# Normalising the attention probabilities of both layers on GpSimd, with a second product by a power of two

## What is computed

```python
q_hk = (hidden_q @ Wq.T).reshape(b, s, H, K)
q_big = jnp.einsum('bshk,hkq->bshq', q_hk, w_kc_q)   # layer 0 also turns q_big by its position
q_r = jnp.einsum('bshq,hqr->bhsr', q_big, W_qr)
k_r = jnp.einsum('bld,hdr->bhlr', kv_rope, W_kr)
scores = jnp.einsum('bhsr,bhlr->bhsl', q_r, k_r)
attn = jax.nn.softmax(scores, axis=-1)
ctx_c = jnp.einsum('bhsl,bld->bhsd', attn, kv_rope)
ctx_lat = jnp.einsum('bhsd,hkd->bshk', ctx_c, w_kc_kv)
out = ctx_lat.reshape(b, s, H * K) @ Wo.T
```

## Time and profile before

| | us |
|---|---|
| median of three runs | 1126.4 |
| lowest and highest | 1124.43, 1128.03 |
| the profiled execution | 1128.36 |
| its span on the core | 1126.6 |

### The profile page before, as it was taken

The page is one execution under the profiler, slowest core; times in us unless marked ns, Lnnn a source line. Parts: engine busy times, 40 slices in busy tenths (PEclk is TensorE's granted clock), DMA queues, the critical chain, the costliest instruction groups (busy, mean ns, idle before and its releaser), DMA issues. The chain is left out here.

```text
span 1126.6 us, 19728 instructions
## 1 busy us (share of the span) xinstructions
PE 989.5 (88%) x6194; PEld 577.9 (51%) x6202; DVE 745.8 (66%) x1315; ACT 542.8 (48%) x1224; POOL 525.5 (47%) x518
## 2 busy tenths in 40 slices
PE   0679999999999998899567569999999988998998
PEld 0335555555555555444233245776777764444543
DVE  3768777777877776396688527888888884323112
ACT  1355656565665656100467316677767673105400
POOL 2968999899899989100233203333333331110000
PEclk9999999999999999999879769999999999999999
DMA  7112121303212110350300002121221003204000
GB/s 218 56 43 66 44 72 36 98 19 98 64 43 65 42 28 21 140 190 35 112 10 19 29 9 71 62 65 65 65 65 59 6 1 140 75 1 159 0 29 37
DMA packets 24191, 69.23 MB, mean 61 GB/s; under 512 B 3162, under 2 KB 5338, under 8 KB 21719
## 3 DMA queue, kind: packets, MB, share of 16 engines
q1 hardware_dynamic: 18656, 58.01, 15.4%
q10 hardware_dynamic: 5492, 10.67, 3.5%
HBM read 64.99 MB, written 3.67 MB: 61 GB/s over the span
## 5 line engine op out<-in xcount | busy, mean ns | idle before, releaser
L819 ACT ACTIVATE scratch<-ps,mxn 112x375 f32<-112x375 f32 x256 | 144.2, 571 | 61.5 <-DVE mxn L940 61.5
L1086 POOL TENSOR_SCALAR scratch<-scratch,rinv 112x375 f32<-112x375 f32 x128 | 164.3, 1293 | 17.0 <-DVE rinv L945 16.7
L1203 PE MATMUL ps<-arena 128*128 128x512 f16 x672 | 147.8, 382 | 2.3 <-PEq L600 2.3
L1075 POOL CAST scratch<-scratch 128x375 f16<-128x375 f32 x128 | 67.1, 524 | 174.3 <-ACT scratch L846 174.3
L940 DVE TENSOR_REDUCE mxn<-ps 112x2 f32<-112x750 f32 x128 | 119.2, 931 | 17.8 <-PE ps L633 17.4
L684 PE MATMUL ps<-xnT,scratch 128*128 128x448 f16 x576 | 124.0, 362 | 3.8 <-DVE scratch L1023 2.4
L671 PE MATMUL ps<-scratch,kvn_hi 125*128 125x224 f16 x768 | 119.9, 260 | 6.8 <-DVE scratch L994 4.7
L656 PEld LDWEIGHTS ps<-ident,scratch 112*125 112x125 f32 x768 | 99.9, 188 | 46.1 <-issue 34.8
L1078 POOL TENSOR_TENSOR scratch<-scratch 128x375 f16<-128x375 f32 x128 | 115.3, 901 | 10.6
L656 PE MATMUL ps<-ident,scratch 112*125 112x112 f32 x768 | 106.7, 275 | 13.7 <-DVE scratch L1014 9.2
L1068 POOL TENSOR_TENSOR scratch<-scratch 128x896 f32<-128x896 f32 x64 | 104.4, 1633 | 27.2 <-DVE scratch L972 26.3
(11 more groups left out here) (138 smaller groups left out, 1538.0 us busy)
## 6 DMA issues: line engine op xcount, KB each, us to landing
scratch<-in_wq SPq DMA_DIRECT2D x16, 512.0 KB, 5.3
scratch<-in_wo SPq DMA_DIRECT2D x16, 512.0 KB, 3.6
wabs<-in_w ACTq DMA_DIRECT2D x32, 256.0 KB, 3.0
scratch<-in_w SPq DMA_DIRECT2D x8, 1024.0 KB, 4.9
scratch<-in_W SPq DMA_DIRECT2D x8, 1024.0 KB, 6.2
scratch<-in_kcq SPq DMA_DIRECT2D x8, 512.0 KB, 5.4
scratch<-in_qr SPq DMA_DIRECT2D x32, 128.0 KB, 3.6
scratch<-in_kcq SPq DMA_DIRECT2D x8, 384.0 KB, 3.3
```

Of the source, the lines that this page charges most:

```text
L819: last = nc.scalar.activation(prob[0:S, s % 2, hh, :], scores_ps[0:S, hh, 0:L], ACT.Exp, bias=mxn[0:S, s % 2, hh:hh + 1], accum_out=rsum[0 ...
L1086: last = nc.gpsimd.tensor_scalar(prob[0:S, s % 2, hh, :], prob[0:S, s % 2, hh, :], rinv[0:S, s % 2, hh:hh + 1], None, ALU.mult)
L1203: last = nc.tensor.matmul(ps[:, b, :], a[:, h, ds(t * P, P)], c[:, h, :], start=(h == 0 and i == 0), stop=(h == H - 1 and i == 2))
```

## The change

In layer 1 NORM leaves VectorE and goes to GpSimd, ahead of K in its list, so that GpSimd normalises in both layers. In both layers GpSimd's instruction now makes two products in one pass, by the reciprocal and by 2^14. The factor 2^14 is taken out of the two instructions behind the transposes: ScalarE's copy has no scale any more, and VectorE's low half becomes a plain difference of two operands.

```diff
 GPSIMD (layer 1)
-    [("K", 2)], [("K", 3)], [("K", 4)], [("K", 5)],
...
+    [NORM, ("K", 2)], [NORM, ("K", 3)], [NORM, ("K", 4)], [NORM, ("K", 5)],
...
 turned_out (ScalarE)
                             probT_hi[0:LP, s % 2, :].rearrange("p (c n) -> p c n", c=LC),
-                            turn_ps[0:LP, :, 0:2 * S], ACT.Copy,
-                            scale=P_SCALE).then_inc(turn_high, 1)
+                            turn_ps[0:LP, :, 0:2 * S], ACT.Copy).then_inc(turn_high, 1)
 reciprocals (VectorE)
-                        if layer == 0:
-                            return
-                        dve.wait_ge(recip_done, nth(p, B, s))
-                        for hh in range(2):
-                            last = nc.vector.tensor_scalar(
-                                prob[0:S, s % 2, hh, :], prob[0:S, s % 2, hh, :],
-                                rinv[0:S, s % 2, hh:hh + 1], None, ALU.mult)
-                        last.then_inc(prob_done, 1)
 turned_low (VectorE)
-                        nc.vector.scalar_tensor_tensor(
+                        nc.vector.tensor_tensor(
                             probT_lo[0:LP, s % 2, :].rearrange("p (c n) -> p c n", c=LC),
-                            turn_ps[0:LP, :, 0:2 * S], P_SCALE,
+                            turn_ps[0:LP, :, 0:2 * S],
                             probT_hi[0:LP, s % 2, :].rearrange("p (c n) -> p c n", c=LC),
-                            ALU.mult, ALU.subtract).then_inc(turn_out, 1)
+                            ALU.subtract).then_inc(turn_out, 1)
 normalise (GpSimd)
                             last = nc.gpsimd.tensor_scalar(
                                 prob[0:S, s % 2, hh, :], prob[0:S, s % 2, hh, :],
-                                rinv[0:S, s % 2, hh:hh + 1], None, ALU.mult)
+                                rinv[0:S, s % 2, hh:hh + 1], P_SCALE, ALU.mult, ALU.mult)
```

More of the change, by code:

```diff
@@ L138 @@
 ], [
-    [("K", 2)], [("K", 3)], [("K", 4)], [("K", 5)],
-    [("K", 6)], [("K", 7)], [("K", 0)], [("K", 1)],
+    [NORM, ("K", 2)], [NORM, ("K", 3)], [NORM, ("K", 4)], [NORM, ("K", 5)],
+    [NORM, ("K", 6)], [NORM, ("K", 7)], [NORM, ("K", 0)], [NORM, ("K", 1)],
 ])
```

## The result

The changed kernel takes 1123.87 us in the median of 14 executions (1120.14 to 1126.12) where the kernel before takes 1126.62 (14 executions, 1124.43 to 1131.51): a ratio of 0.9963, with 95% between 0.9953 and 0.9974. The ratio makes it some 4.2 us; the two medians by themselves are 2.8 us apart. Measured a second time, unaltered, it gave 0.997 (0.9957 to 0.9983; experiment 7). The forecast was 9.9 us. The time lies inside the range, but less than half of the forecast gain is there.

A forecast was written before the change was run, and what follows sets the result against it. TensorE sets the pace, with GpSimd close behind in layer 0 and VectorE in layer 1. Terms 2.1 + 6.0 + 1.0 + 0.8 = 9.9 us took the median from 1126.4 to 1116.5; range 1112 to 1127.

The forecast's parts named there:

- The instruction: GpSimd's NORM instruction with two products, 375 elements: 0.52 us, between 0.36 and 0.89, where one product takes 1.29.
- Rivals 1 and 2: GpSimd's two-product instruction keeps its price: 1126 us, chance 0.13; or pays for each product: about 1340, with milder forms 0.10.
- rival 1: GpSimd's instruction keeps its price; layer 1's last slots take 3.86 us, last transposes 0.8 later; 1126 us, chance 0.13.
- Layer 0, middle pairs: Six middle pairs of layer 0: TensorE does not wait for NORM, so a quicker GpSimd changes nothing, 0 us.
- Layer 0, the end: Last pair of layer 0: slots shrink from 3.86 to 3.35 us and last transposes start 0.8 earlier, 2.1 us gained.
- Layer 1: Layer 1 without NORM on VectorE: 6.0 us from the pairs, 1.0 at the start, 0.8 in the last pair.
- The pair: Each pair of layer 1 shortens by 0.91 us through three slots, for 7 pairs, some weaker: 6.0 us.
- slot 6: Layer 1, where Q's halves stand behind NORM on VectorE: TensorE starts S earlier, 0.33 us back a pair.
- W's slot: Layer 1, three VectorE products between NORM and the low half: 0.28 us back a pair.
- the slot with U: Layer 1, slot behind slot 6: VectorE would start U's low half 0.25 us earlier, 0.30 back a pair.
- The other two edits: Factor removed from VectorE's difference out of PSUM and scale from ScalarE's copy, both layers: 0 us.
- own range: Whole kernel: 1112.5 to 1121 us, allowing a third of layer 1's gain lost or another 3 us of hidden stalls.

The follow-up runs named there:

- experiment 7: The whole change measured a second time, unaltered, against the kernel before: 1124.37 us against 1127.33, ratio 0.997.
- experiment 3: NORM on GpSimd in both layers with one product, factor 2^14 kept behind the transposes, against the kernel before: 1130.73 us, ratio 1.0027.
- experiment 4: Two kernels without the model, copying the input and running GpSimd's forms alone and beside VectorE's split: one product of 375 columns 1.22 us, two products 0.59.
- experiments 1 and 2: The change in layer 0 alone: 1127.18 us, ratio 1.0004; the change in layer 1 alone: 1122.41 us, ratio 0.996; both against the kernel before.
- 5 for the path: VectorE's second weight split moved behind the maxima in the changed kernel: 1113.24 us; moved ahead of U instead: 1114.0; behind the maxima in the kernel before: 1120.2.

## Why the prediction was wrong, point by point

**The instruction** was forecast at 0.52 us, between 0.36 and 0.89; it takes 0.59 undisturbed, 0.62 in the mean. The reading that the two-operation form is the cheap one held, for two products too. Rivals 1 and 2 fell with it, and experiment 3 shows that rival 1 had the slots at the end of layer 1 right (3.86 us), but not what is lost behind them (2.6 us until the projection starts, where it had 0.8). By the rule of the Trainium skill, "GPSIMD Engine Reference", section "Elementwise — side-by-side cycle accounting", one and two operations cost the same; experiment 4 has 1.22 against 0.59 us, which contradicts it.

**Layer 0, middle pairs: the failed step.** The prediction says "In the middle pairs TensorE waits for VectorE and ScalarE there and not for NORM, so I count 0 (the cover is TensorE's own work, 97%)". The first half was true and should have been the alarm. TensorE waited for VectorE once in each pair, so whatever makes VectorE later there costs the path at once. The step asked only whether a quicker GpSimd gives something back, and took no change to be the worst case. But it moves every GpSimd instruction behind NORM earlier, onto another instruction of VectorE. The cost is 0.37 us in six pairs and 0.15 in the first, 2.4 us in all (experiments 1 and 2 for where it comes from, 4 for the mechanism, 5 for the path). A middle pair that grows was in none of the rivals.

**Layer 0, the end** was forecast at 2.1 us and gave 2.2: the last slots went to 3.35, 3.36 and 3.35 us (1.34) and the last transposes came 0.84 earlier. No scores wait for GpSimd any more, as said.

**Layer 1.** 7.8 us were forecast, 6.5 came. The start gave 1.04 for 1.0, the end 0.76 for 0.8. The pair gave 0.69 of 0.91: slot 6 gave 0.35 for 0.33, W's slot 0.31 for 0.28, and the slot with U 0.04 for 0.30. This last term was mis-sized. It took VectorE to start U as soon as ScalarE is through. ScalarE (858) and VectorE (980), first in the loop, then in the pair that is written out:

```profile
771.83 0.62 ACT L858 ACTIVATE arena<-ps 128x512 f32 x1
```

```profile
772.71 0.69 DVE L980 SCALAR_TENSOR_TENSOR arena<-ps,arena 128x512 f32 x1 [0.92 <-ACT arena L858]
```

```profile
708.24 0.61 ACT L858 ACTIVATE arena<-ps 128x512 f16<-128x512 f32 x1
```

```profile
708.89 0.69 DVE L980 SCALAR_TENSOR_TENSOR arena<-ps,arena 128x512 f16<-128x512 f32 x1 [0.70 <-ACT arena L858]
```

VectorE begins 0.26 us after ScalarE's end in the loop and 0.04 in the written-out pair. Before the change it began 0.31 after, and the prediction put all of that down to NORM. In the loop the address of U's result depends on the pair and is worked out in two instructions between the wait and line 980; in the written-out pair it is a constant, and there the slot did give 0.19. The trace of the changed kernel has this everywhere: all 24 instances of line 980 in the loops of both layers start 0.24 to 0.27 us behind ScalarE's end, 7 of the 8 written-out ones 0.03 or 0.04 (the first found VectorE busy), and in layer 1's loop line 985, which has nothing between its wait and its work, starts 0.02 to 0.04 behind ScalarE where it waits for it. It could have been read before: in layer 0's loop, where VectorE has no NORM, the 12 instances of line 989 begin 0.24 to 0.26 us behind ScalarE. That those two instructions are the 0.22 us is argued from these places; it was not tried by itself.

**The other two edits** cost 0, as said: the low half takes 847 ns where it took 846.

**The sum.** 9.9 forecast, less 2.4 for the slot in layer 0, less 1.3 in layer 1, and 0.1 more at layer 0's end, is 6.3 us in the attention (6.2 with all digits). Timed were 4.2 and 3.4 by the ratios, 2.8 and 3.0 by the medians. The other 2 to 3 us go with the lower granted clock behind layer 1: 1.7 us of it are shown where the projection starts at half speed, in those executions that have it, and that the rest is the clock too is argued. The mean clock is lower in every kernel with NORM moved in layer 1 (0.965 to 0.969) than in every one without (0.970 or 0.971); why is open, since the one cause that was tried did not bear out. The prediction had no term for it, and its "own range" of 1112.5 to 1121 was too narrow for lack of both. That 1123.87 lies in the stated range is owed to its width, which had to take in rival 1, and not to the sum.

## What to carry to other kernels

A step made quicker on GpSimd moves what GpSimd does next; before counting it as free, look in the timeline at which of its instructions will then be under way when VectorE starts one with two operands in SBUF, and whether TensorE waits for that VectorE instruction anywhere. An instruction of VectorE that nobody waits for does not belong ahead of maxima that everybody waits for: that one entry was worth more (6.8 us) than the change as it was measured (3 to 4 us). And before moving an elementwise product to GpSimd, give it a second operation if there is one to be had: it halves the instruction.

## What was unexpected of the hardware

- GpSimd's product by a value for each row takes 1.22 us for 375 elements with one operation and 0.59 with two, whether the second is a product or a sum; on 1024 elements 2.85 and 1.12.
- VectorE's split of 128x1024 from two SBUF operands takes 1.22 us alone, 1.41 when it starts in a GpSimd cast, 1.53 in two products, 1.83 in a difference, up to 1.88 in the kernel; GpSimd stands meanwhile. Beside two products VectorE's difference out of PSUM keeps its 0.85 us.
- The mean granted clock of the whole span is 0.970 or 0.971 where VectorE normalises layer 1's softmax and 0.965 to 0.969 where GpSimd does; the cause is open. Half speed where the projection starts costs 1.7 us.
- VectorE starts 0.24 to 0.27 us behind ScalarE where two address instructions stand between its wait and its work, and 0.03 us where none does.
